# Two 32-wide attentions: scores once with queries on partitions, P scaled on GpSimd and turned on TensorE

## The reference

```python
def _L0_attn_ref(x, Wq, Wk, Wv, Wo):          # 16 query heads share 4 key/value heads
    q = (x @ Wq).reshape(B, S, N_KV, GROUP, HEAD_DIM)
    k = (x @ Wk).reshape(B, S, N_KV, HEAD_DIM)
    v = (x @ Wv).reshape(B, S, N_KV, HEAD_DIM)
    scores = jnp.einsum('bqkgd,bskd->bkgqs', q, k) * scale
    scores = jnp.where(causal, jnp.finfo(scores.dtype).min, scores)
    attn = jax.nn.softmax(scores, axis=-1)
    out = jnp.einsum('bkgqs,bskd->bqkgd', attn, v)
    return out.reshape(B, S, N_EMBD) @ Wo
...
    x = x + _L0_attn_ref(_layernorm(x, axis=-1), L0_attn_Wq, L0_attn_Wk, L0_attn_Wv, L0_attn_Wo)
```

## Time and profile before

| | us |
|---|---|
| median of 3 runs | 3494.19 (3494.19 to 3494.88) |
| the profiled execution | 3500.92 |
| its span | 3498.6 |
| PE busy in the span | 3095.8 (88%) |
| DVE busy | 1945.1 (56%) |
| ACT busy | 1294.4 (37%) |
| POOL busy | 707.5 (20%) |

### The profile page before, as it was taken

How to read it: one execution, slowest core, us unless ns; L and a number is a source line. 1 busy time by engine, 2 the same in 40 slices (tenths; PEclk the granted TensorE clock), 3 DMA queues, 4 the chain that set the end, 5 groups by cost and what they waited for, 6 DMA issues and landing times. The chain is left out here.

```text
span 3498.6 us, 50867 instructions
## 1 busy us (share of the span) xinstructions
PE 3095.8 (88%) x19076; PEld 2333.1 (67%) x19076; DVE 1945.1 (56%) x5124; ACT 1294.4 (37%) x2672; POOL 707.5 (20%) x873
## 2 busy tenths in 40 slices
PE   6999899997999995978868866998779999989999
PEld 4777677886667663445556754776367777768887
DVE  5555387776444445323466668664677777752221
ACT  2333266664323323123322225442545555531000
POOL 1111032221101100000027760000033333313222
PEclk8999999998999997878989987999889999999999
DMA  2000031112000003111110020001200000020000
GB/s 88 2 2 2 4 124 32 32 32 73 1 1 1 1 2 124 40 59 62 63 58 4 4 77 22 1 1 52 96 1 1 1 1 1 1 100 13 13 13 13
DMA packets 66456, 106.41 MB, mean 30 GB/s; under 512 B 9379, under 2 KB 30115, under 8 KB 66085
## 3 DMA queue, kind: packets, MB, share of 16 engines
q1 hardware_dynamic: 65798, 103.07, 8.4%
q0 software_dynamic: 416, 0.10, 0.0%
HBM read 90.40 MB, written 12.85 MB: 30 GB/s over the span
## 5 line engine op out<-in xcount | busy, mean ns | idle before, releaser
L402 ACT ACTIVATE tree_value<-tree_bit,table_lut,tree_step 128x256 f32<-128x256 uint8 x496 | 275.4, 595 | 139.6 <-DVE tree_value L416 68.8
L416 DVE COPY_PREDICATED tree_value<-tree_bit,tree_value 128x256 f32<-128x256 uint8 x434 | 233.3, 542 | 137.9 <-ACT tree_value L402 108.7
L805 DVE CUSTOM_DVE_ANT_0 bank<-bank,a_causal 128x384 f32<-128x384 f32 (+3 forms) x512 | 235.5, 523 | 117.3 <-PE bank L921 117.3
L729 ACT ACTIVATE a_PT<-bank 128x512 f32<-128x512 f32 (+1 forms) x384 | 174.4, 527 | 314.9 <-PE bank L934 314.9
L101 PE MATMUL bank<-f_xT_hi,f_w_hi 128*128 128x512 f32 (+1 forms) x704 | 276.5, 393 | 8.1 <-DVE f_w_lo L1219 8.1
L102 PE MATMUL bank<-f_xT_hi,f_w_lo 128*128 128x512 f32 (+1 forms) x704 | 276.0, 392 | 0.0
L103 PE MATMUL bank<-f_xT_lo,f_w_hi 128*128 128x512 f32 (+1 forms) x704 | 275.8, 392 | 0.0
L1143 POOL CAST f_h_hi<-f_sg 128x512 fp32r<-128x512 f32 (+1 forms) x88 | 85.8, 975 | 544.4 <-DVE f_sg L1240 273.0
L1242 DVE TENSOR_TENSOR f_sg<-bank,f_sg 128x512 f32<-128x512 f32 (+1 forms) x44 | 30.4, 691 | 271.3 <-PE bank L103 271.3
L101 PEld LDWEIGHTS bank<-f_xT_hi,f_w_hi 128*128 128x128 f32 (+1 forms) x704 | 132.7, 188 | 37.6 <-issue 8.7
L103 PEld LDWEIGHTS bank<-f_xT_lo,f_w_hi 128*128 128x128 f32 (+1 forms) x704 | 132.5, 188 | 28.9
(11 more groups left out here) (468 smaller groups left out, 8050.4 us busy)
## 6 DMA issues: line engine op xcount, KB each, us to landing
f_w_raw<-in_f_w SPq DMA_DIRECT2D x11, 768.0 KB, 12.1
f_w_raw<-table_w SPq DMA_DIRECT2D x11, 768.0 KB, 11.8
tree_idx<-in_f_idx SPq DMA_DIRECT2D x62, 128.0 KB, 2.1
table_w<-tree_value SPq DMA_DIRECT2D x62, 128.0 KB, 1.7
x_res<-in_x SPq DMA_DIRECT2D x4, 1024.0 KB, 10.8
m_piece<-in_m_wq SPq DMA_DIRECT2D x2, 2048.0 KB, 12.0
m_piece<-in_m_wo SPq DMA_DIRECT2D x2, 2048.0 KB, 8.3
m_piece<-in_m_w_gate SPq DMA_DIRECT2D x2, 2048.0 KB, 10.9
```

What stands on the lines that cost most here:

```text
L402: act.activation(prog.tree_value[(h + to) % 4][:, :], prog.tree_bit[h % 2][0][:, :], ACT.Identity, bias=prog.table_lut[:, 2 * k:2 * k + 1] ...
L416: dve.copy_predicated(prog.tree_value[(h + keep) % 4][:, :], prog.tree_bit[h % 2][bit][:, :], prog.tree_value[(h + other) % 4][:, :]).then ...
L729: act.activation(PT[j][:, g, :], ps[J.bank(key)][:, 0:WIDTH[j]], ACT.Exp, scale=scale).then_inc(J.frees(key), 1)
L805: last = dve.tensor_tensor_reduce(out=ps[J.bank(key)][:, col:col + n], in0=ps[J.bank(key)][:, col:col + n], in1=causal[:, T - n:T], scale= ...
```

## The change

In `attention32` alone:

- Scores are made once, with queries on partitions, in chunks: chunk j of a unit holds the parts [(0, 3)], [(0, 2), (384, 0)] or [(0, 1)] (column, query tile), for four heads; four PSUM banks, two heads at a time.
- DVE (`low`) adds the mask, multiplies by minus the scale and takes the row minimum in the same one pass, from PSUM into SBUF (`Pr`).
- ACT (`exp`) takes exp in place in SBUF with the row minimum as bias and scale -1, and its accumulator gives the row sums.
- DVE takes the reciprocal of the sums (at most 128x8), POOL multiplies the chunk in place by it.
- PE turns 128x128 tiles by transposes (`PT`, ten groups of four heads per unit), ACT copies each group out of PSUM, PE multiplies by V tile by tile (`PV`), ACT copies O, POOL writes OT (a0: hi and lo; a1: a copy).
- The second score pass, the row-maximum term, the mask products, the maxima's transposes, the products for sums and spreading, and two constants (`c_sums`, `c_spread`) go. `ORDER`, `pieces` and the banks are laid out anew; the projections and Y are the same products.

```diff
+    NPT = 4
+    PT = [prog.sb(f"{name}_PT{i}", [P, G * P], F32) for i in range(NPT)]
+    O = [prog.sb(f"{name}_O{i}", [P, T], F32) for i in range(2)]
...
+    S_BANK, PT_BANK, O_BANK, PIECE = 0, 4, 6, 7
...
+    for n in range(CHUNKS):
+        m, j = n // 3, n % 3
+        b, u = UNITS[m]
+        near, far = pieces(b, u, j)
+        groups = range(FIRST[n], LAST[n] + 1)
+        if n and n + 2 < CHUNKS:
+            ORDER += [(("low", n + 2, 0), 0), (("low", n + 2, 1), 0)]
+        if n + 1 < CHUNKS:
+            ORDER.append((("rec", n + 1, 0), 0))
+        if n and n + 2 < CHUNKS:
+            ORDER += [(("low", n + 2, 2), 0), (("low", n + 2, 3), 0)]
+        for half in range(2):
+            some = groups[2 * half:2 * half + 2]
+            ORDER += [(("PT", i, 0), PT_BANK + i % 2) for i in some]
+            ORDER += [(("PV", i - 2, 0), 0) for i in some if i >= 2]
+            if j == 0 and half == 0 and m:
+                ORDER.append((("O", m - 1, 0), O_BANK))
+                if UNITS[m - 1][1] > 1:
+                    ORDER.append((("OT", m - 1, 0), 0))
+            if n + 2 < CHUNKS:
+                ORDER += [(("exp", n + 2, g), 0) for g in (2 * half, 2 * half + 1)]
+            if half == 0:
+                ORDER += [(piece, PIECE) for piece in near]
+        if n + 3 < CHUNKS:
+            ORDER.append((("S", n + 3, 0), 0))
+        ORDER += [(piece, PIECE) for piece in far]
+        if n + 3 < CHUNKS:
+            ORDER.append((("S", n + 3, 1), 0))
...
         def _(pool):
+                elif kind == "rec":
+                    j = at % 3
+                    pool.wait_ge(*c_rec(0, at + 1))
+                    for g in range(G):
+                        for i, (col, qt) in enumerate(PARTS[j]):
+                            n = (qt + 1) * P
+                            last = pool.tensor_scalar(Pr[j][:, g, col:col + n], Pr[j][:, g, col:col + n], rec[:, j, i, g:g + 1], None, ALU.mult)
+                    last.then_inc(c_scaled.sem, 1)
...
         def _(act):
+                elif kind == "exp":
+                    j = at % 3
+                    act.wait_ge(*read(("S", at, k)))
+                    for i, (col, qt) in enumerate(PARTS[j]):
+                        n = (qt + 1) * P
+                        last = act.activation(Pr[j][:, k, col:col + n], Pr[j][:, k, col:col + n], ACT.Exp, bias=low[:, j, i, k:k + 1], scale=-1.0,
+                                              accum_out=total[:, j, i, k:k + 1])
+                    last.then_inc(c_exp.sem, 1)
+                elif kind == "PT":
...
+                    if at >= NPT:
+                        act.wait_ge(*used(at - NPT))
+                    act.activation(PT[at % NPT][:, :], ps[J.bank(key)][:, :], ACT.Copy).then_inc(J.frees(key), 1)
...
         def _(dve):
+                elif kind == "low":
+                    j = at % 3
+                    if k == 0 and at >= 3:
+                        dve.wait_ge(*full(("PT", LAST[at - 3], 0)))
+                        dve.wait_ge(*full(("PT", LAST[at - 3] - 1, 0)))
...
+                        last = dve.tensor_tensor_reduce(out=Pr[j][:, k, col:col + n], in0=ps[J.bank(source)][:, col:col + n], in1=causal[:, T - n:T],
+                                                        scale=-scale, scalar=-NEG, op0=ALU.add, op1=ALU.min, accum_out=low[:, j, i, k:k + 1])
+                elif kind == "rec":
+                    j, parts = at % 3, len(PARTS[at % 3])
+                    dve.wait_ge(*c_exp(0, G * (at + 1)))
+                    dve.reciprocal(rec[:, j, 0:parts, :], total[:, j, 0:parts, :]).then_inc(c_rec.sem, 1)
...
         def _(pe):
+                elif kind == "PT":
+                    m, j, col, qt, kt = GROUPS[at]
+                    if at == FIRST[3 * m + j]:
+                        pe.wait_ge(*c_scaled(0, 3 * m + j + 1))
+                    pe.wait_ge(*vacant(key))
+                    for g in range(G):
+                        last = pe.transpose(ps[J.bank(key)][:, g * P:(g + 1) * P], Pr[j][:, g, col + kt * P:col + (kt + 1) * P], prog.ident[:, :])
```

More of the change, by code:

```diff
@@ L523, in attention32 @@
-    LAST_PRODUCT = lambda b: ("Q" if KC == 1 else "K", b, 3)
[L524 to L532, removed]
+    UNITS = [(b, u) for b in range(NB) for u in range(DC)]
@@ L533, in attention32 @@
+    LAST_PRODUCT = lambda b: ("Q" if KC == 1 else "K", b, 3)
+    S_BANK, PT_BANK, O_BANK, PIECE = 0, 4, 6, 7
+    ORDER = [(("T", 0, c), 4 + c) for c in range(DC)] + [(("Q", 0, 0), 4), (("K", 0, 0), 5)]
     if biased:
         ORDER.append((("const", 0, 0), 7))
[L535 to L560, removed]
-            for i, piece in enumerate(pieces(b, u, k)):
-                ORDER.append((piece, EXP_BANK + (i + (k == 3)) % 3))
@@ L563, in attention32 @@
-    end = UNITS[-1]
-    ORDER += [(("pv", end, 2), 0), (("sum", end, 2), 0), (("bc", end, 0), SUM_BANK)] + [(("Y", end[0], k), EXP_BANK + k % 3) for k in range(4)]
+    if KC == 1:
+        beside = [[(("VT", 0, 0), 6)], [(("V", 0, 0), 7)], [(("Q", 0, 1), 4)]]
+    else:
+        beside = [[(("V", 0, 0), 6), (("V", 0, 1), 4)], [(("Q", 0, 1), 5), (("V", 0, 2), 6)], [(("K", 0, 1), 7), (("V", 0, 3), 4)]]
+    for n in range(3):
+        ORDER += [(("S", n, 0), 0), (("S", n, 1), 0)] + beside[n] + [(("low", n, g), 0) for g in range(G)]
+        if n < 2:
+            ORDER += [(("exp", n, g), 0) for g in range(G)]
+        if n == 0:
+            ORDER.append((("rec", 0, 0), 0))
@@ L569, in attention32 @@
     QK_NO = {key: i + 1 for i, key in enumerate(key for key in ORDER if key[0] in ("Q", "K"))}
     jobs = []
+    opened = set()
     for kind, at, k in ORDER:
-        if kind in ("max", "exp"):
-            base = MAX_BANK if kind == "max" else EXP_BANK
-            jobs += [((kind, at, f), base + f % 3) for f in range(3 * k, 3 * k + 3)]
-        elif kind == "pv" and k == 0:
-            jobs += [(("O", at), O_BANK), (("sum", at), SUM_BANK)]
-        elif kind not in ("pv", "sum"):
+        if kind == "S":
+            jobs += [(("S", at, g), S_BANK + g) for g in (2 * k, 2 * k + 1)]
+        elif kind == "PV":
+            m = at // PER
+            if m not in opened:
+                opened.add(m)
+                jobs.append((("O", m, 0), O_BANK))
+        elif kind not in ("low", "exp", "rec", "O", "OT"):
@@ L841, in _ @@
                 elif kind == "Y":
-                    key = (kind, at, k)
                     t = at * TT + k
@@ L893, in _ @@
+                    last.then_inc(J.fills(key), 1)
+                elif kind == "S":
+                    (b, c), j = UNITS[at // 3], at % 3
+                    if j == 0 and k == 0:
                         pe.wait_ge(*read(("Q", b, c)))
                         pe.wait_ge(*read(("K", b, c % KC)))
-                    if kind == "exp" and k == 0:
-                        pe.wait_ge(*read(("rows", at, 0)))
-                        if unit(at) == 0:
-                            pe.wait_ge(*c_init(0, n_init))
-                            pe.wait_ge(*c_const(0, 16 * n_const))
@@ L929, in _ @@
-                    for f in some:
-                        j, g = FILLS[f]
-                        out = ps[J.bank((kind, at, f))]
-                        if kind == "exp":
-                            for col, t in T_PARTS[j]:
-                                last = pe.matmul(out[:, col:col + P], prog.mask_b[:, 1, :], prog.ident_b[:, :], start=False, stop=True,
-                                                 skip_group_check=True)
-                            last.then_inc(J.fills((kind, at, f)), 1)
-                elif kind == "rows":
-                    key = (kind, at, 0)
-                    pe.wait_ge(*c_nm_lo(0, unit(at) + 1))
+                    some = (2 * k, 2 * k + 1)
@@ new lines, in _ @@
+                    pe.wait_ge(*read(("PT", at, 0)))
+                    for g in range(G):
+                        strip = slice(HD * g, HD * (g + 1))
+                        v = V[b % 2][:, kt, (c % KC) * P + HD * g:(c % KC) * P + HD * (g + 1)]
+                        last = pe.matmul(ps[J.bank(out)][strip, qt * P:(qt + 1) * P], v, PT[at % NPT][:, g * P:(g + 1) * P],
+                                         start=at % PER == 0, stop=kt == qt, skip_group_check=True)
+                    last.then_inc(J.fills(out) if at % PER == PER - 1 else c_pv.sem, 1)
+                elif kind == "Y":
+                    if k == 0:
+                        pe.wait_ge(*c_ot(0, DC * (at + 1)))
+                        if at == 0 and split_y:
+                            pe.wait_ge(*c_wlo(0, 4))
```

339 lines of the change are left out of this document (111 added, 228 removed).

## The result

| | before | after |
|---|---|---|
| median, us | 3494.53 (3494.19 to 3497.00, 4 runs) | 3522.03 (3518.75 to 3531.91, 4 runs) |
| ratio after to before, 95% | | 1.0082 [1.0061, 1.0102] |
| profiled execution, its span | 3500.92, 3498.6 | 3521.41, 3519.6 |

A forecast was written before the change was run, and what follows sets the result against it. PE was taken to bound the two attentions before the change. a0 gains 6 us and a1 51 plus 2 of tail, together 57; less 16 for waits, net 41; 3500.9 - 41 - 6.7 = 3453 us, range 3345 to 3545.

The forecast's parts named there:

- PE's saving: PE work per unit in both attentions: 11.9 us replace 16.6, 4.7 less; PE alone would pace 19.6 (a0), 25.3 (a1).
- ACT, DVE: Per unit, ACT 16.8 us (a0) and 17.9 (a1), exponentials 8.5, row-sum reads overlapping; DVE 12 or less; both under PE.
- POOL's price: POOL's sixteen in-place multiplies per unit: 18.3 us at 2.9 ns a column; 22.4 by the upper row.
- rival C: POOL multiplies at the upper row, 3.7 ns a column: period 26.5 us in both attentions, 3528 us; chance 0.18.
- rival B: POOL multiplies near the cast's rate, so PE paces both attentions: 117 us less, 3377 us; chance 0.33.
- The new loop: Wait circle of scaling, reciprocal and scores: POOL's period 6.8 + 7.7 + 8.8 = 23.3 us in a0, under PE's 25.3 in a1.
- The first O: First copy of O after filling the pipeline: at 63 us in a0 (64 with POOL), at 902 in a1.
- The last two units: Units without products at each attention's end: POOL paces them at 21.4 us each in a0, 21.9 in a1.
- The waits given back: Allowance for waits the new order adds in both attentions: 0.5 us a unit, 16 us.
- Rival D: PE's gaps while POOL scales bring the half clock: period 29.9 us, a0 87 more, a1 14 more, 3595 us; chance 0.13.
- The prediction's own sign for it: Listed as what would make the forecast wrong: a clock under 0.9 in the two attention stretches.
- A: Main case: POOL multiplies at 2.9 ns a column in both attentions, 3453 us, alone 3420 to 3490; chance 0.36.

The follow-up runs named there:

- e9: Changed kernel with the second projection product or transpose between two bodies moved behind later scores, first two mask passes and reciprocal; POOL scaling: 3542.82 us, 1.0138 to before.
- e11: Changed kernel with two heads scaled on DVE, two on POOL, and the far pieces moved behind the mask passes and reciprocal: 3405.89 us, 0.9748 to before.
- e3: Changed kernel with forty 128-column bf16 products put on PE ahead of its wait for each unit's first scaled chunk: 3518.30 us, 1.0054 to before.
- e4: Changed kernel with all scaling of P moved from POOL to DVE, right behind the reciprocal: 3406.44 us, 0.9736 to before.
- e7: Changed kernel with heads 0 and 1 scaled on DVE behind the reciprocal, the other two on POOL: 3398.40 us, 0.9722 to before.
- e12: Changed kernel with heads 0 to 2 scaled on DVE behind the reciprocal, the last on POOL: 3392.33 us, 0.9709 to before.
- e2: Changed kernel with the reciprocal of chunk n+2 moved right behind its exponentials, ahead of chunk n+3's scores: 3531.77 us, 1.0094 to before.

## Why the prediction was wrong, point by point

- **PE's saving**: right. 19.6 and 25.3 us a unit forecast, 19.4 and 25.1 with the scaling all but gone. Inside it, errors cancel: a pair of turns and P·V takes 1.54 us (285.64 to 287.18), not 1.37, and two heads' scores of the middle chunk 1.0 us each time, but the first chunk's four heads together only 0.9 (287.18 to 288.09), as much as two heads alone where a piece stands between the halves (1175.82 to 1176.71 in a1). The excess of 0.17 a pair goes the way of the rule on mode changes (the Trainium skill, TensorEngine Tiling (Array Packing), Key Properties), though no run separates it.
- **ACT, DVE**: right enough. The exponentials take 8.8 us a unit for 8.5, the row-sum reads do overlap them (two exponentials start 0.60 us apart, 299.53 and 300.13, with a read of 0.19 between), and in a0 ACT is busy for 63%, DVE for 40%.
- **POOL's price**: right, 17.3 for 18.3 us a unit; rival C fell with it, though its 3528 is the number nearest to the result. The range reached up to 3545 for C's sake, so that the time lies inside it is luck. The page that puts GpSimd roughly at line rate for one input (the Trainium skill, GPSIMD Engine Reference, Engine selection), on which rival B leaned, doesn't hold for this instruction: 1574 ns at 512 columns, where the cast takes 612.
- **The new loop** is the step that failed: "POOL's period is 6.8 + 7.7 + 8.8 = 23.3 us in a0", and under PE's 25.3 in a1. The last term holds only without a far piece (8.9 us); with one it is 11 to 12. And the middle term must be the longer of POOL's scaling of the middle chunk, with what stands ahead of it on POOL, and what PE does from the first chunk's turns to the middle's: 8.5 us in a0, 12.3 in a1. I followed the circle along POOL and left out PE's side of it, the far pieces and DVE's pass on them. That is 25.3 against 23.3 in a0 (26 us in 13 units) and 28.6 against 25.3 in a1 (42 us). In a0 the copies of O tell the causes apart: the seven units without a far piece take 23.7 us on average, near the forecast, and the six with one 27.2, which is 23 of the 26 us. That the far pieces are the cause is read from these rows; the runs moved them (e9, e11), and none took them away. PE's side is the longer one in a0 only by the half clock (8.5 us, 7.0 in e3), in a1 by the far piece in leg 2.
- **The first O**: forecast 27 us (a0) and 41 us (a1) after the first scores; it came at 76.4 for 64, and 51.8 after them in a1 (they start at 891.0): 12 and 11 us more. The last products of a unit stand behind the next unit's first turns, and so behind another wait for scaling.
- **The last two units**: 36.6 (a0) and 35.0 us (a1) in place of 42.8 and 43.8, 15 us less than forecast. Each copy of O but the last stands behind the first turns of the next unit, which is also in the 12 and 11 us above; the last doesn't, and in a0 the two take 24.6 and 12.0 us.
- **The waits given back**: 16 us were set aside for what the new order adds. The above makes 26 + 42 + 12 + 11 - 15 = 76, less those 16: 60 us above the forecast for the profiled execution (3459.9), which took 3521.4: 61.5 above.
- **Rival D**: its mechanism is there, its price isn't. The prediction's own sign for it came, a clock of 0.87 in a0. The slow stretch after each wait (3.6 us, 280.64 to 284.25) lies in leg 2 of the circle, and without it a0 is 12 us shorter, where D had put 93 us between itself and A (87 more for 6 less). D's 3595 can't be retraced to the last us; 13 units at 29.9 with the other terms of A give 3599.

## What to carry to other kernels

When work moves off the bounding engine to an idle one, busy times say only what the floor is. Write the new circle of waits as legs, and where two engines can close a leg (here POOL's scaling and PE's in-order work in between) take the longer one, unit by unit, with every piece that an in-order queue holds inside the leg. In this circle the slow engine cost a fifth of its time up to the slack and three fifths above it; sharing its work with an engine that already sits next in the chain (here DVE, behind its own reciprocal) gave up to 2.9%, while each mere reordering moved the wait to another engine or changed nothing.

## What the runs showed of the hardware

VectorE and GpSimd slow each other when both multiply in SBUF. DVE's multiply with all scaling on it (e4), the same beside POOL (e7), and POOL's with three heads on DVE (e12):

```profile
L815 DVE TENSOR_SCALAR a_P<-a_P,a_rec 128x512 f32<-128x512 f32 x128 | 53.6, 483 | 1.1
```

```profile
L821 DVE TENSOR_SCALAR a_P<-a_P,a_rec 128x512 f32<-128x512 f32 x64 | 41.7, 695 | 1.1
```

```profile
L661 POOL TENSOR_SCALAR a_P<-a_P,a_rec 128x512 f32<-128x512 f32 x32 | 67.4, 2107 | 188.6 <-DVE a_rec L816 188.6
```

483 ns become 695, and POOL's 1574 become 2107. The split of xT, two SBUF inputs on DVE, takes 1082 ns in the changed kernel and 878 in e4, where POOL has no scaling; in e2, where POOL scales as much but the order differs, it takes 879.

The mask pass, whose first input is in PSUM, isn't touched (678 ns in the changed kernel, 686 in e4). The Trainium skill (SBUF — State Buffer, Who interferes with whom) says that DVE and GpSimd share a pair of ports that one of them holds for a whole instruction when DVE uses two ports, and that its instructions with two SBUF inputs contend with GpSimd's reads; the rows agree as to which instructions grow, though means over many don't show whether one waits for a whole instruction of the other. The prediction hadn't looked at this. It is small here: 6 us for the xT passes in all.
